# Third expert layer: one set of moments for two normalisations, shorter shares, and a state normalised on ScalarE

## The reference

```python
def _L2_ffn_ref(hidden_states, ...):                     # hidden_states = layernorm(x)
    def _layer_norm(x, w, b):
        mu = jnp.mean(x, axis=-1, keepdims=True)
        var = jnp.mean(jnp.square(x - mu), axis=-1, keepdims=True)
        return (x - mu) * jax.lax.rsqrt(var + LN_EPS) * w + b
    ln1 = _layer_norm(hidden_states, ln1_weight, ln1_bias)
    ...                                                  # q, k, v; 16 heads, causal over the 8 states
    h1 = hidden_states + proj
    x = _layer_norm(h1, ln2_weight, ln2_bias).reshape(-1, H)
    probs = jax.nn.softmax(x @ router_weight, axis=-1)   # 8 experts
    top_p, top_i = jax.lax.top_k(probs, 2)
    top_p = top_p / jnp.sum(top_p, axis=-1, keepdims=True)
    ...                                                  # at most 640 rows an expert, in order of rows
    fc1 = jax.nn.gelu(jnp.einsum('ech,ehf->ecf', xt, moe_w1))
    fc2 = jnp.einsum('ecf,efh->ech', fc1, moe_w2)
    return h1 + moe_out                                  # the two experts' rows by their shares
```

## Time and profile before

| what | us |
|---|---|
| median of 3 runs | 1466.97 (1464.44 to 1469.62) |
| the profiled execution, its own time | 1471.18 |
| its span, first to last instruction | 1469.4 |
| TensorE busy, whole span | 1193.6 |
| VectorE busy | 1054.7 |
| ScalarE busy | 728.8 |
| POOL busy | 418.9 |
| mean granted clock of TensorE | 0.906 of full |

### The profile page before, as it was taken

The page is one execution under the profiler, slowest core; times in us unless marked ns, Lnnn a source line. Parts: engine busy times, 40 slices in busy tenths (PEclk is TensorE's granted clock), DMA queues, the critical chain, the costliest instruction groups (busy, mean ns, idle before and its releaser), DMA issues.

```text
span 1469.4 us, 26756 instructions
## 1 busy us (share of the span) xinstructions
PE 1193.6 (81%) x9106; PEld 834.7 (57%) x9106; DVE 1054.7 (72%) x2951; ACT 728.8 (50%) x1186; POOL 418.9 (29%) x645
## 2 busy tenths in 40 slices
PE   5989888999978777767778783777788999978887
PEld 3766667888843333356344442666676444437776
DVE  7878866666666777547898985687875666647886
ACT  5454523333236667646676772443333566634442
POOL 5545431000142333014555432132313323200110
PEclk9999998999977999978798886899888999988999
DMA  8000000000000000000000000000000000000000
GB/s 333 1 1 1 1 1 1 0 0 0 0 1 1 1 0 1 1 1 1 1 2 0 1 2 0 1 1 1 1 1 1 2 2 0 1 1 1 1 1 29
DMA packets 5846, 14.57 MB, mean 10 GB/s; under 512 B 240, under 2 KB 4464, under 8 KB 5360
## 3 DMA queue, kind: packets, MB, share of 16 engines
q1 hardware_dynamic: 5744, 13.26, 2.4%
HBM read 12.21 MB, written 1.05 MB: 9 GB/s over the span
## 4 chain that ended last, share of the span: by engine, by line
issue 36%; PE 30%; DVE 15%; POOL 5%; DVEq 5%; ACT 4%; POOLq 4%; DMA 1%; SPq 0%; ACTq 0%
PE PS L1840 5%; PE PS L1849 3%; PE PS L1254 3%; PE PS L1202 2%; PE PS L1196 2%; PE PS L1179 2%; PE PS L1404 2%; PE PS L1094 2%; POOL trs L412 1%; DVE mx L2123 1%; POOLq L411 1%; PE PS L1093 1%; PE PS L1071 1%; POOL hrs L412 1%; DVE sbuf L2030 1%
## 5 line engine op out<-in xcount | busy, mean ns | idle before, releaser
L2123 DVE TENSOR_REDUCE mx<-PS 128x2 f32<-128x512 f32 (+1 forms) x256 | 155.6, 620 | 82.1 <-PE PS L1202 73.3
L727 ACT ACTIVATE w_l0f<-PS 128x512 f32<-128x512 f32 (+1 forms) x256 | 137.2, 543 | 102.5 <-PE PS L1209 99.6
L410 POOL TENSOR_TENSOR tve<-tmv,eps 128x2 f32<-128x2 f32 x64 | 15.3, 240 | 513.8 <-DVE tmv L1911 317.3
L1840 PE MATMUL PS<-hT_padded,w_l0f 128*128 128x256 f32 x512 | 122.8, 386 | 0.0
L1840 PEld LDWEIGHTS PS<-hT_padded,w_l0f 128*128 128x128 f32 x512 | 95.1, 195 | 11.2
L1003 ACT ACTIVATE sg<-PS 128x512 f32<-128x512 f32 x64 | 38.2, 597 | 120.8 <-PE PS L1840 120.7
L1556 PE MATMUL PS<-w_l2f,y 128*128 128x128 f32 x512 | 77.8, 301 | 14.7 <-DVE acc L2405 8.2
L1556 PEld LDWEIGHTS PS<-w_l2f,y 128*128 128x128 f32 x512 | 74.1, 214 | 22.3 <-ACT y L839 12.0
L3046 DVE TENSOR_TENSOR y<-sg,PS 128x512 f32<-128x512 f32 x64 | 44.0, 687 | 50.9 <-ACT sg L1003 43.7
L2217 DVE SCALAR_TENSOR_TENSOR w_l0f<-w_l0f 128x768 f32<-128x768 f32 x64 | 67.0, 1046 | 11.3 <-ACT w_l0f L784 10.4
L1196 PE MATMUL PS<-w_cbf 128*128 128x384 bf16 x256 | 69.9, 342 | 5.8 <-DVE mx L2123 2.7
(11 more groups left out here) (495 smaller groups left out, 3264.6 us busy)
## 6 DMA issues: line engine op xcount, KB each, us to landing
w_l0f<-in_l0f SPq DMA_DIRECT2D x1, 3076.0 KB, 18.2
w_l2f<-in_l2f SPq DMA_DIRECT2D x1, 2214.0 KB, 18.9
w_l3f<-in_l3f SPq DMA_DIRECT2D x1, 1736.0 KB, 22.5
w_l0a<-in_l0a SPq DMA_DIRECT2D x1, 960.0 KB, 7.5
result<-X SPq DMA_DIRECT2D x1, 896.0 KB, 4.6
X<-in_x SPq DMA_DIRECT2D x1, 768.0 KB, 11.4
w_l1f<-in_l1f SPq DMA_DIRECT2D x1, 582.0 KB, 14.8
PT<-in_cbf SPq DMA_DIRECT2D x1, 576.0 KB, 9.2
```

The lines of the kernel that those rows point to most:

```text
L727: act.activation(P8[:, hh % 8, 0:width], PS[:, hh % 2, 0:width], ACT.Exp, scale=SM_SCALE).then_inc(a["pt"], 1)
L1840: ins = pe.matmul(PS[:, 2 * (c % 2) + g, b * L:(b + 1) * L], w("l0f", "w1")[:, at:at + P], hT[:], start=True, stop=True)
L2123: dve.tensor_reduce(mx[:, hh, 0:nm], PS[:, 2 + hh % 2, 0:nm * keys].rearrange("p (t k) -> p t k", t=nm), AX.X, ALU.max).then_inc(a["mx"], 1)
```

## The change

1. The inner normalisation no longer reads `H1`. With the variance v of a row of `X`, both normalisations together are (x - mean) times one factor, (v (1 + EPS) + EPS^2)^-0.5. VectorE's `inner_stats`, `inner_moments` and `inner_norm` go, and POOL's `inner_rstd`.
2. `state_rstds` on POOL takes the place of `outer_rstd` and `inner_rstd`: it makes both factors by one power over four columns, and an offset -mean x factor. Before the power it waits for `m_n1`, that is for the state normalised before. The start now also takes the moments of unit 0 from `X`.
3. `inner_norm` is on ScalarE: two ACTIVATEs with a scale and a bias a row, in the loop after Gelu 4 of iteration i for unit i + 3, and in the start after `short_load`.
4. The gate's first sum, reciprocal and product go. The exponentials themselves are compared, and `chosen` takes them; the sum over the two that are kept follows as before.
5. `rk` is signalled by `counted`, ahead of combine 5 and of the reciprocal.

```diff
-        mhalf = sb("mhalf", [P, T])
+        mhalf2 = sb("mhalf2", [P, 2 * T])
+        mhalf = mhalf2[:, 0:T]
...
-                    def outer_rstd(u):
-                        rstd(m_xst, m_xrs, u, xmv, xve, xrs)
+                    def state_rstds(u):
+                        pool.wait_ge(m_xst, u + 1)
+                        pool.tensor_tensor(xve[:, 0:T], xmv[:, :, 1], eps[:], ALU.add)
+                        pool.tensor_scalar(xve[:, T:2 * T], xmv[:, :, 1], 1.0 + EPS, EPS * EPS, ALU.mult, ALU.add)
+                        pool.tensor_scalar(xneg[:], xmv[:, :, 0], -1.0, None, ALU.mult)
+                        pool.drain()
+                        if u:
+                            pool.wait_ge(m_n1, u)
+                        pool.tensor_tensor(xrs[:], xve[:], mhalf2[:], ALU.pow)
+                        pool.drain()
+                        pool.tensor_tensor(xnm[:], xneg[:], xrs[:, T:2 * T], ALU.mult).then_inc(m_xrs, 1)
...
-                    inner_rstd(0)
-                    outer_rstd(1)
-                    inner_rstd(1)
-                    outer_rstd(2)
+                    state_rstds(0)
+                    state_rstds(1)
+                    state_rstds(2)
                     all_key_products(0)
-                    inner_rstd(2)
                     all_value_products(0)
...
-                            outer_rstd(i + 3)
-                            inner_rstd(i + 3)
+                            state_rstds(i + 3)
...
+                    def inner_norm(u):
+                        act.wait_ge(m_xrs, u + 1)
+                        if u:
+                            act.wait_ge(m_tr, u)
+                        for t in range(T):
+                            ins = act.activation(n1[:, t, :], X[:, u * T + t, :], ACT.Identity,
+                                                 scale=xrs[:, T + t:T + t + 1], bias=xnm[:, t:t + 1])
+                        ins.then_inc(m_n1, 1)
...
+                    inner_norm(0)
                     inner_copy(0)
                     short_load(0)
+                    inner_norm(1)
                     short_exp(0)
                     inner_copy(1)
                     short_load(1)
+                    inner_norm(2)
                     short_copy(0)
...
+                            if c == 4 and there(i + 3):
+                                inner_norm(i + 3)
...
                     def compared(u):
-                        other = own8(u).unsqueeze(2).to_broadcast([P, T, E8, E8])
-                        own = own8(u).unsqueeze(3).to_broadcast([P, T, E8, E8])
+                        dve.wait_ge(f["gx"], u + 1)
+                        other = e8.unsqueeze(2).to_broadcast([P, T, E8, E8])
+                        own = e8.unsqueeze(3).to_broadcast([P, T, E8, E8])
...
-                        dve.tensor_tensor(cum1[:], cum[:], mbf[:, 0, :], ALU.add)
+                        dve.tensor_tensor(cum1[:], cum[:], mbf[:, 0, :], ALU.add).then_inc(f["rk"], 1)
...
                         combine(i, 2)
...
-                        if N:
-                            inner_stats(n)
                         if G:
                             gate_max(g)
                         dve.drain()
                         if G:
                             gate_less(g)
-                        if N:
-                            inner_moments()
                         combine(i, 3)
...
                             value_products(dve, s, 0)
                             value_products(dve, s, 1)
-                        if G:
-                            gate_sum(g)
-                        dve.drain()
-                        if G:
-                            gate_inverse()
-                        if N:
-                            inner_norm(n)
-                        dve.drain()
-                        if G:
-                            gate_parts(g)
-                        if S:
                             value_products(dve, s, 2)
-                        dve.drain()
                         if G:
                             compared(g)
                         combine(i, 4)
...
                         combine(i, 5)
                         dve.drain()
                         if G:
-                            gate_inverse().then_inc(f["rk"], 1)
+                            gate_inverse()
```

More of the change, by code:

```diff
@@ L257, in block_program @@
         m_ld, m_kp, m_vp = sem("m_ld"), sem("m_kp"), sem("m_vp")
-        m_xst, m_xrs, m_st, m_rs, m_n1, m_tr, m_n1T, m_qkv, m_sc, m_ex, m_ao, m_aT, m_aTs, m_y = (
-            sem("m_" + n) for n in "xst xrs st rs n1 tr n1T qkv sc ex ao aT aTs y".split())
+        m_xst, m_xrs, m_n1, m_tr, m_n1T, m_qkv, m_sc, m_ex, m_ao, m_aT, m_aTs, m_y = (
+            sem("m_" + n) for n in "xst xrs n1 tr n1T qkv sc ex ao aT aTs y".split())
         run = RUN
@@ L411, in rstd @@
                 pool.drain()
-                pool.tensor_tensor(rs[:], ve[:], mhalf[:], ALU.pow).then_inc(ready, 1)
+                pool.tensor_tensor(rs[:], ve[:], mhalf, ALU.pow).then_inc(ready, 1)
             def head_rstd(count):
@@ L418, in tail_rstd @@
                 rstd(tl_stat, tl_rstd, count, tmv, tve, trs)
-            pool.memset(mhalf[:], -0.5)
+            pool.memset(mhalf2[:], -0.5)
             pool.memset(eps[:], EPS)
@@ L2258, in hidden_state @@
                     def hidden_state(u):
-                        dve.wait_ge(m_xrs, u)
+                        dve.wait_ge(m_xrs, u + 1)
                         for t in range(T):
@@ L2262, in hidden_state @@
                                               xmv[:, t, 0:1], xrs[:, t:t + 1], ALU.subtract, ALU.mult)
-                    def inner_stats(u):
-                        for t in range(T):
-                            dve.bn_stats(nst[:, t, :], H1[:, u * T + t, :])
-                    def inner_moments():
-                        for t in range(T):
-                            ins = dve.bn_aggr(nmv[:, t, :], nst[:, t, :])
-                        ins.then_inc(m_st, 1)
-                    def inner_norm(u):
-                        dve.wait_ge(m_rs, u + 1)
-                        for t in range(T):
-                            ins = dve.tensor_scalar(n1[:, t, :], H1[:, u * T + t, :], nmv[:, t, 0:1],
-                                                    nrs[:, t:t + 1], ALU.subtract, ALU.mult)
-                        ins.then_inc(m_n1, 1)
                     mine = range(T * NG - POOL_GROUPS)
@@ L2359, in gate_less @@
                         dve.tensor_tensor(lg[:, :, 0:E8], g8, over8(gmx), ALU.subtract).then_inc(f["ge"], 1)
-                    def gate_sum(u):
-                        dve.wait_ge(f["gx"], u + 1)
-                        dve.tensor_reduce(gsm[:], e8, AX.X, ALU.add)
                     def gate_inverse():
                         return dve.reciprocal(gsm[:], gsm[:])
-                    def gate_parts(u):
-                        dve.tensor_tensor(own8(u), e8, over8(gsm), ALU.mult)
                     def compared(u):
-                        other = own8(u).unsqueeze(2).to_broadcast([P, T, E8, E8])
-                        own = own8(u).unsqueeze(3).to_broadcast([P, T, E8, E8])
+                        dve.wait_ge(f["gx"], u + 1)
+                        other = e8.unsqueeze(2).to_broadcast([P, T, E8, E8])
+                        own = e8.unsqueeze(3).to_broadcast([P, T, E8, E8])
                         dve.tensor_tensor(square(eqb), other, own, ALU.is_equal)
@@ L2421, in _ @@
                     dve.tensor_copy(H1[:, 0:T, :], h[:])
+                    outer_stats(0)
+                    dve.drain()
+                    outer_moments()
+                    dve.drain()
                     outer_stats(1)
                     dve.drain()
-                    inner_stats(0)
+                    dve.wait_ge(m_xrs, 1)
                     outer_moments()
                     dve.drain()
-                    inner_moments()
+                    outer_stats(2)
                     hidden_state(1)
                     dve.drain()
-                    inner_norm(0)
-                    inner_stats(1)
-                    outer_stats(2)
-                    dve.drain()
-                    inner_moments()
                     outer_moments()
@@ L2440, in _ @@
                     short_max(0)
-                    inner_norm(1)
                     hidden_state(2)
```

22 lines of the change are left out of this document (3 added, 19 removed).

## The result

The changed kernel takes 1462.37 us (median of nine runs, 1449.93 to 1464.49), the kernel before beside it 1469.21 us (median of nine, 1463.11 to 1473.53): a ratio of 0.9941, with a 95% interval from 0.9916 to 0.9966. It is faster by more than the 0.3% that a measurement tells. The forecast was 1459.0, with 1453 to 1465. The profiled execution took 1462.57 us.

What follows compares the result with a forecast made beforehand. No engine is full; waits ending at combine 4 and at `ao` bound the kernel. 7.8 us over the loop plus 0.2 in the start make 8.0 off: median 1467.0 to 1459.0, range 1453 to 1465.

Steps and rivals of the forecast that it cites:

- Combine 4 in iterations 0 and 2: Combine 4 then starts on down 4's end: gain 0.92 us in iteration 0, 1.05 in iteration 2.
- Iteration 1: Combine 4, counted on VectorE: third value product starts where the sum did, 968.13 instead of 969.32, gain 1.19 us.
- Iterations 3 and 4: Combine 4 waits for down 4: 1.85 us, or 1.4 if a hole returns; 1.65 taken for each.
- Iteration 5: Combine 4, with no second normalisation there: 1075.19 instead of 1075.90, gain 0.7 us.
- The signal for the ranks: Earlier rk: worth nothing of its own in iterations 0 to 5, 0.63 us in iteration 6.
- ScalarE's pair: Two ACTIVATEs per state after Gelu 4: 0.8 us taken, covered by 0.7 before down 5, so costing nothing.
- POOL's power over four columns: On POOL, in the chain from moments to factor: 0.69 to 1.2 us, with 0.4 to 0.9 of cover.
- The start: Up to the first combine: 0.2 us shorter, between 0.35 longer and 0.75 shorter.
- Rival 1, the clock: TensorE's clock moves: three more slow places give 1464, three fewer 1454; better 0.14, worse or rival 3 0.18.
- a sign of being wrong: Iterations whose granted clock moved by more than 0.1 would show the prediction wrong.
- Rivals 2 and 3: 2: all iterations at clock 0.74, 1479, chance 0.06. 3: ScalarE's or POOL's work on path, 1465, 0.18 with clock worse.
- The other signs: TensorE's rank wait falls to nothing, its ao wait grows to 1 to 2.4 us; waiting for Gelu 5 means wrong.

Runs made afterwards that it cites:

- stats_back: Changed kernel with two statistics put back ahead of the gate's maximum and the aggregates behind its subtraction, read by nobody: 1460.11 us.
- both_back: Changed kernel with the gate's first sum, reciprocal and product and the second normalisation both back on VectorE: 1465.04 us.
- shares_back: Changed kernel with only the gate's first sum, reciprocal and product put back ahead of the comparison: 1459.15 us.
- norm_dve: Changed kernel with the second normalisation made by VectorE at its old place, ScalarE's pairs gone: 1461.71 us.
- rk_back: Changed kernel with only the rank signal put back, behind combine 5 with the gate's second reciprocal: 1464.53 us.
- start: Changed kernel with the start reordered, POOL's first key products ahead of its third factor: 1457.69 us.
- pow2: Changed kernel with POOL's power over four columns done twice, the first into a spare tile: 1461.67 us.
- aofirst: Changed kernel with combine 5 moved behind short_share, so that ao comes earlier: 1457.26 us.
- after: The changed kernel itself in its first profiled execution, against the kernel before: 1462.57 us.
- same: The repeated run: changed kernel again, unaltered; 1459.31 us (six runs) against 1471.35 for the kernel before, ratio 0.9917.

## Why the prediction came true, and where it didn't

- **Combine 4 in iterations 0 and 2** (0.92 and 1.05): right, 0.95 and 1.04, at mean clocks of 0.98 to 1.00, with combine 4 starting on down 4's end. stats_back and both_back give the two parts in iteration 0: 0.17 and 0.89 (the prediction had put the first at nothing there). In iteration 2 they don't add up by themselves: both_back gives 0.15, and the statistics 0.39 in the like iterations 1 and 4; the rest needs all the removed work on VectorE at once, as the kernel before has it.
- **Iteration 1** (1.19): gained 2.16. The step took combine 3 as it stood before, at 965.98, and counted from there on VectorE. But that combine had waited 2.06 us for a down 3 in a slow stretch:

```profile
965.98 0.61 DVE L2405 SCALAR_TENSOR_TENSOR acc<-PS,cwn,acc 128x128 f32<-128x128 f32 x2 [2.06 <-PE PS L1556]
```

  At the full clock the slack is on VectorE in this iteration too, and down 4 decides (shares_back and norm_dve change nothing there). The step had the wrong limit. The size beyond it goes with the clock (0.86 before, 1.00 now), less 0.37 for a hole that came up ahead of combine 2.
- **Iterations 3 and 4** (1.65 each): 2.26 and 3.83. From combine 2 to combine 4, iteration 4 went from 5.96 to 4.34, 1.62 less: the step was right. The other 2.26 lie from combine 4 to combine 7 (10.80 to 8.54): 1.90 of them are a wait of 3.33 for down 7 in a slow stretch before, which is 1.43 now, and 0.34 are a hole at 1050.99 that is gone. Iteration 3 is the right number for a wrong reason in this execution: combine 3 to combine 4 fell by 2.29 (4.65 to 2.36), 1.10 of it is given back before combine 3 by a slow stretch that lies there now, and combine 4 waits for VectorE and not, as forecast, for down 4. Combine 4 comes 1.19 earlier, and 1.32 more lie from there to combine 7, where the slow stretch of before is gone. At the full clock, in the repeated run, the step holds as written: 6.20 from combine 2 to combine 4 before (a hole of 0.43 in it), 4.35 there, 1.85 less.
- **Iteration 5** (0.7): 0.31. shares_back puts 0.74 back at combine 4, so the step is right; a hole of 0.45 without a releaser came up before the reciprocal and took half. The prediction allowed for such a hole in iteration 3 alone.

```profile
1074.80 0.17 DVE L2369 RECIPROCAL gsm<-gsm 128x2 f32<-128x2 f32 x1 [0.45 <-issue]
```

- **The signal for the ranks** (nothing in six, 0.63 in iteration 6): right in both; rk_back has 0 in iterations 1 and 4 and 0.78 in 6. The remaining 0.26 of that iteration's 1.04 is a hole that vanished.
- **ScalarE's pair** (0.8, covered): 0.87 and covered. By the Trainium skill's formula ("ScalarE: Activation LUTs", section "What ACT_TABLE_LOAD costs") the estimate had been 0.87, and the trace agrees. For the row of 558 ns, which has two pointer operands, the same formula gives an estimated 585: it agrees within 5%, less closely than the prediction says.
- **POOL's power over four columns** (0.69 to 1.2): 1.02, covered in the loop by 0.55 or more.
- **The start** (0.2, bounds -0.35 to 0.75): outside its bounds, 1.07, and 1.12 in the repeated run. Up to `short_add(0)` the working held: POOL's first key products came 1.17 later (9.14 to 10.31 after the copy; 0.35 to 1.5 was allowed), and `short_add(0)` 0.30 earlier (18.30 to 18.00; from 0.6 later to 0.5 earlier was allowed). What failed is the claim that only a quarter us follows. Before, a hole of 0.43 stood ahead of POOL's power for the head, and VectorE's head normalisation took 0.74 beside POOL's products. The hole is gone, and the normalisation takes 0.60 beside the same products (which take 0.89 instead of 0.80). That makes 0.30 become 0.73 where the head's state reaches ScalarE. Of the further 0.34, 0.11 is the rank signal (rk_back); the rest stays open.
- **Rival 1, the clock.** It moved in both directions: the excess of iterations 1, 3 and 4 over their terms is 0.97 + 0.61 + 2.18 = 3.76 us, most of it slow stretches and 0.34 a hole, and the identical instructions outside the layer lost 3.96. They cancel in this pair by luck, which is why the total (8.7 of span for 8.0) looks better than its parts. The mean clock of iterations 1 and 4 moved by 0.14 and 0.11, more than the 0.1 that the prediction gave as a sign of being wrong, so one profile against the other can't prove the sum; what the offsets bear out is the steps at combine 4 in iterations 2, 3 and 4, one by one. What the prediction draws from the earlier trace rows, that busy time doesn't sort full and lower clock, isn't shown: the 20.6 us of TensorE are themselves long because of the lower clock. Over the nine runs of the same code the time goes with the mean granted clock: 1449.93 us at 0.921, 1457.21 at 0.918, 1464.49 at 0.911. **Rivals 2 and 3** fell: no iteration became slower, and the new work is covered in the loop. In the start it stands on the path (start and pow2), as the working had it.
- **The other signs.** TensorE never waited for Gelu 5. Its wait for the ranks went in iterations 0 to 4 and 6, but 1.38 of it stayed in iteration 5. Its wait for `ao` became 0.45, 0.78, 1.12, 1.76, 1.77 and 2.65 in iterations 0 to 5, wider than the 1 to 2.4 forecast.

So the mechanism was right where the clock was full, with 8.0 us against 6.8 between the medians of one comparison and 12.0 of the other (1471.35 to 1459.31). The 1459.0 was reckoned from a median of three runs; from the 1469.21 of the nine beside it, 8.0 less would be 1461.2.

## What to carry to other kernels

Removing work from the engine that looks fullest gains only up to the next chain that ends at the same point: work out the slack at that point first, then remove what stands on the chain (here two statistics of 0.39 us ahead of the gate counted in full, while 0.7 us behind it counted for nothing in two iterations and for 0.09 in a third). A signal sent earlier is worth nothing where the same engine next waits for something that is not earlier. And a small edit under a clock that moves by itself is judged by offsets within a stretch at full clock, not by one execution's time.

## What the runs showed of the hardware

- Holes of 0.35 to 0.45 us without any releaser stand before some instructions of VectorE and POOL. They belong to the program and not to the execution: the changed kernel has one at 966.73 and one at 1074.80, and the repeated run has both before the same instructions. They move when instructions are added or removed elsewhere: those that the kernel before had in iterations 3 and 4 are gone, and the one at 966.73 is gone in shares_back, norm_dve and aofirst, where combine 2 of iteration 1 comes 0.37 earlier. What makes them, no run here shows. They are as large as many of the terms above.

```profile
966.73 0.29 DVE L2304 TENSOR_TENSOR sc<-sc,mx 128x128 f32<-128x128 f32 x1 [0.45 <-issue]
```

- A power on POOL took 0.69 over two columns and 1.02 over four.
- In two executions of one program the stretches at the lower clock lay in different iterations; that moved iteration 2 by 1.07 us and iteration 4 by 1.67 (after and same).
